# Integer cross attention of a decoder kernel: 128-row scores from queries beside zeros, and the first half of the scores issued twice

## The chip, the cores and the metric

The kernel runs on one core of a Trainium2 chip. The metric is the device time of one execution in microseconds, from the first to the last instruction and the little around them; lower is better. TensorE is written PE, VectorE DVE, ScalarE ACT, GpSimd POOL and SyncE, which issues the DMAs, SP.

## What is computed

The program is a decoder of four layers on `x` of shape (4, 256, 256) in float32, each layer with a self attention, a cross attention on `ctx_2048` (4, 256, 256) and a feed-forward block. The change touches only the cross attention of the second layer (stage "l1x"). Its reference, cut to what matters:

```python
q = (x @ Wq + bq).reshape(1, B * N, 16, 16)          # 1024 queries, 16 heads of 16
kv = (cond @ Wkv + bkv).reshape(1, -1, 2, 16, 16)    # 1024 keys and values
q, k, v = q * 0.25, kv[:, :, 0], kv[:, :, 1]
q = fq_sym(q, axis=-1)     # round to whole numbers -127..127 times a scale
k = fq_sym(k, axis=-1)
v = fq_sym(v, axis=2)
attn = softmax(q @ k.T)
attn = fq_unsigned(attn)   # whole numbers 0..255 times a scale
out = (attn @ v) @ Wp + bp
```

Every query of the four batches attends to all 1024 keys.

## The kernel before, in words

The 1024 queries are 8 tiles of 128 rows, and a tile has 16 heads, so the stage is 128 steps, numbered n = 16·tile + head; a head of its tile is called step h below. At line 1567 `at(n)` gives both. What a step does, engine by engine:

- **PE** (`tensor`, lines 1607 to 1642). Two products (line 1618) write the scores of one head, 128 queries by 1024 keys, into one of three double banks `wide[n % 3]`. The stationary operand is the tile's turned queries, the moving one the turned keys `kt`. A head takes 64 rows of these, four slots of 16: the whole-number query is repeated in each slot, and the slots of the key hold the scaled key cut into three bfloat16 parts and zeros. Two heads share the 128 rows, so the products take rows 0 to 63 for an even head and 64 to 127 for an odd one (`r`, line 1610). A score waits for the exponentials of step n-3 (line 1616), which free its bank. Then PE mixes the values of step n-7 (line 1628): eight products of 128 rows and 16 columns, which wait for POOL's whole probabilities (line 1623). At h = 9 of the next tile it turns a finished tile's output (line 1632), at h = 11 it multiplies it with `Wp` (line 1637, four float32 products of 256 columns) once ACT has copied the turned output (line 1754). PE takes all of this in this one order. The products are issued in the helper at line 101, the transposes in the one at line 107.
- **DVE** (`vector`, lines 1680 to 1707): the maximum over 1024 scores (line 1684) and a small operation on it (line 1686); at h = 7 the reciprocal and scaling of the tile before (lines 1689, 1694); at h = 12 the sum into the residual and its statistics (lines 1699 to 1703).
- **ACT** (`scalar`, line 1748): the exponentials of 1024 scores as bytes, and the copy of line 1754. After every second tile it normalizes a batch for the block that follows (line 385).
- **SP** (`sync`, lines 1813 to 1823): turns the bytes by a DMA transpose (line 1823), once exponentials n and POOL's step n-6 are done. At h = 4 it turns the next tile's queries (line 1797) by another transpose.
- **POOL** (`gpsimd`, lines 1783 to 1793): widens the turned bytes to bfloat16 (line 1787, "whole"), adds a bias at h = 4 (line 1791), and at h = 7 after every second tile it computes the normalization's scale (lines 346 to 358), for which it waits for DVE's statistics of h = 12.

Each engine's program is written in order, with waits on semaphores; there is no planner in this stage. After the loop the items of the following feed-forward block run (PE lines 1640 to 1642: float32 products of 256 columns). Queries lie in `arena_a`, two buffers of 512 words per row; the untransposed keys `kx` lie in `big_b` and are dead once the keys are turned (line 1800).

Of the kernel before, what the change touches and what calls it, by code (L numbers as in the profile page):

```python
# [11 lines left out]
BF16 = mybir.dt.bfloat16  # L12
# [6 lines left out]
P = 128  # L19
NB, S, D = 4, 256, 256  # L20
TB = S // P
NT = NB * TB
CB = TB * D
KH = D // P
H = 16
# [105 lines left out]
def build(nc, d, out):  # L131
# [1388 lines left out]
    def l1_cross():  # L1520
        s = "l1x"
# [4 lines left out]
        mx, ls, rl = wk.take(NT * H), wk.take(NT * H), [wk.take(H) for _ in range(2)]  # L1526
        c = Cut(arena_a)
        kt = [c.take(NT * P, BF16) for _ in range(H // 2)]
        qt_ = [c.take(H // 2 * P, BF16) for _ in range(2)]
        ca = Cut(arena_a, c.at)  # L1530
        nf = l1x_nf
        kr = [ca.take(512) for _ in range(NB)]
# [56 lines left out]
        def tensor():  # L1589
            def queries(b):  # L1590
                t.wait_ge(*(yield xt_a, s, b))
                for i in range(TB):
                    ins = products(t, banks[4 + b].f[:, i * D:(i + 1) * D], with_row(xt, b, i, lambda k: W["wq4"][:, k * D:(k + 1) * D], W["bq4"]))
                ins.then_inc(*ts.up(s, "q", b))

            yield from queries(0)
            yield from norm_tensor(s, nf, last_bank, [3], by_scalar=True)
            yield from queries(1)
            yield from queries(2)
            yield from queries(3)  # L1600
            for k in range(KH):
                t.wait_ge(*(yield vs, s, "values", k))
                for c in range(2):
                    z = 2 * k + c
                    turns(t, id_b, [(banks[z].h[:, i * P:(i + 1) * P], vq[:, value_keys(k * 2048 + c * 512, i)]) for i in range(4)]).then_inc(*ts.up(s, "vi", z))
            yield MEET
            for n in range(N + 14):
                if n < N:
                    i, h = at(n)
                    r = slice(64 * (h % 2), 64 * (h % 2) + 64)  # L1610
                    if h == 0:
                        t.wait_ge(*(yield q_t_d[i % 2], s, i))
                    if i == 0 and h % 2 == 0:
                        t.wait_ge(*(yield k_t_d[h // 2], s))
                    if n >= 3:
                        t.wait_ge(*(yield exped, s, n - 3))
                    for c in range(2):
                        ins = products(t, wide[n % 3][:, c * 512:(c + 1) * 512], [(qt_[i % 2][r, h // 2 * P:(h // 2 + 1) * P], kt[h // 2][r, c * 512:(c + 1) * 512])])
                    ins.then_inc(*scored.up(s, n))
                if 0 <= n - 7 < N:  # L1620
                    u = n - 7
                    i, h = at(u)
                    t.wait_ge(*(yield gs, s, "whole", u))
                    if h == 0 and i >= 2:
                        t.wait_ge(*(yield added, s, i - 2))
                    if h == 0 and i >= 3 and i % 2:
                        t.wait_ge(*(yield xt_a, "l1f", (i - 3) // 2))
                    products(t, out_bank(i)[:, h * HD:(h + 1) * HD],
                             [(pt[u % 6][:, j * P:(j + 1) * P], vi[:, h * HD + j * D:h * HD + j * D + HD]) for j in range(NT)]).then_inc(*mixed.up(s, u))
                if (i := ended_at(n - 10)) is not None:  # L1630
                    t.wait_ge(*(yield normed_o, s, i))
                    turns(t, id_f, [(out_bank(i)[:, D + j * P:D + (j + 1) * P], oc[i % 2][:, j * P:(j + 1) * P]) for j in range(KH)]).then_inc(*o_in_psum.up(s, i))
                if (i := ended_at(n - 12)) is not None:
                    t.wait_ge(*(yield o_t_a, s, i))
                    if i == 0:
                        t.wait_ge(*(yield as_, s, "weights"))
                    products(t, out_bank(i)[:, 0:D], [(ot[i % 2][:, j * P:(j + 1) * P], wp[j]) for j in range(KH)]).then_inc(*out_made.up(s, i))
                if (b := batch_ended_at(n - 19)) is not None:
                    yield from norm_tensor("l1f", big_a, odd_bank, [b], by_scalar=True)
                if n in (128, 132):  # L1640
                    yield from some(items_tensor, 1)
            yield from some(items_tensor, ALL_ITEMS)
# [117 lines left out]
        def gpsimd():  # L1760
# [22 lines left out]
            for n in range(N):  # L1783
                g.wait_ge(*(yield p_t_d[n % 6], s, n))
                if n >= 6:
                    g.wait_ge(*(yield mixed, s, n - 6))
                g.tensor_scalar(pt[n % 6].rearrange("p (j e q) -> p j e q", j=NT // 2, e=2), by_byte(p8[n % 6]), 1.0, 0.0,  # L1787
                                ALU.mult, ALU.add).then_inc(*gs.up(s, "whole", n))
                if n % H == 4:
                    x_i = x[:, n // H * D:(n // H + 1) * D]  # L1790
                    g.tensor_tensor(x_i, x_i, W["bp4"], ALU.add).then_inc(*gs.up(s, "bias", n // H))
# [2 lines left out]
            yield from ffn_gpsimd()  # L1794

        def turn_queries(i):
            sp.dma_start(qt_[i % 2].rearrange("p (r q) -> p r q", r=H // 2), qx[:, i * 1024:(i + 1) * 1024], transpose=True).then_inc(*q_t_d[i % 2].up(s, i))

        def turn_keys(pr):
            sp.dma_start(kt[pr].rearrange("p (i c) -> p i c", i=NT), kx[:, pr * 1024:(pr + 1) * 1024], transpose=True).then_inc(*k_t_d[pr].up(s))  # L1800
# [1 line left out]
        def sync():  # L1802
# [10 lines left out]
            for n in range(N):  # L1813
                i, h = at(n)
                if h == 4 and i + 1 < NT:
                    sp.wait_ge(*(yield gs, s, "spread", (i + 1) // TB))
                    if i:
                        sp.wait_ge(*(yield scored, s, i * H - 1))
                    turn_queries(i + 1)
                sp.wait_ge(*(yield exped, s, n))  # L1820
                if n >= 6:
# [1940 lines left out]
```

## Time and profile before

| | |
|---|---|
| median of 3 runs | 1644.3 us (1640.3 to 1646.01) |
| the profiled execution | 1643.9 us, span 1642.6 us |
| mean granted PE clock over the span | 0.891 of 2.4 GHz |
| busy | PE 1428.1 us (87%), DVE 1096.7 (67%), ACT 796.2 (48%), POOL 752.1 (46%) |
| the 128 steps, first score to last maximum | about 615 to 823 us |
| maximum over the scores, L1684 | x128, 1214 ns each |
| exponentials, L1748 | x128, 1204 ns each |
| bytes to whole numbers, L1787 | x128, 1045 ns each |

Times in the profile count from the first instruction. A PE matmul is pipelined: its duration holds its way through the array, and in a run of matmuls the next one starts before the last has ended, so what a matmul costs is read from the starts. The granted clock is 1.00 for 2.4 GHz and 0.50 for 1.2 GHz. "Idle before" names what released an engine that had stood still.

### The profile page before, as it was taken

The numbers are of one execution on the slowest core, as the hardware profiler recorded it, in microseconds if no ns is written. First come the engines' busy times: TensorE is split into PE (matmuls) and PEld (weight loads), VectorE is DVE, ScalarE is ACT, GpSimd is POOL, SyncE is SP. The second block draws the span as 40 slices with busy tenths as digits, with TensorE's granted clock in tenths as the row PEclk, the third lists the DMA queues.
The fourth block names the chain that finished last, engine by engine and source line by source line (L and its number), as shares of the span: only waits on it lengthen the run. The fifth ranks groups of instructions, "written<-read, shape, count | busy, mean of one in ns | idle before, by whom it ended". The sixth has DMA issues, their size and how long they took to land. (4 is left out here: it accounts for less than half of the span.)

```text
span 1642.6 us, 25782 instructions
## 1 busy us (share of the span) xinstructions
PE 1428.1 (87%) x8360; PEld 1030.2 (63%) x8360; DVE 1096.7 (67%) x2831; ACT 796.2 (48%) x2003; POOL 752.1 (46%) x1214
## 2 busy tenths in 40 slices
PE   6999997889999988999999698556888777789999
PEld 4666764578888852333377587434666555568887
DVE  6877776357677669889845735675866588954222
ACT  3444442143434358788721624456777477741111
POOL 3888882056656646766712122434656423320000
PEclk9999997899999995555599899769999989999999
DMA  7000002100000016555450000020423264310000
GB/s 274 26 8 8 1 1 77 45 15 7 1 8 1 1 27 116 92 98 85 89 197 1 0 1 0 4 109 15 64 53 60 45 154 108 61 14 1 7 7 13
DMA packets 168836, 77.87 MB, mean 47 GB/s; under 512 B 156928, under 2 KB 161408, under 8 KB 167552
## 3 DMA queue, kind: packets, MB, share of 16 engines
q1 hardware_dynamic: 168704, 76.23, 19.9%
q8 instruction: 68, 1.11, 0.3%
q14 instruction: 64, 0.52, 0.1%
HBM read 37.40 MB, written 1.05 MB: 23 GB/s over the span
## 5 line engine op out<-in xcount | busy, mean ns | idle before, releaser
L101 PE MATMUL banks<-normed_t,arena_a 128*128 128x256 f32 x1120 | 257.3, 385 | 2.5 <-PEq L3667 2.5
L464 POOL TENSOR_TENSOR lut_weights<-lut_weights,arena_b 128x536 f32<-128x536 f32 x128 | 181.5, 1418 | 122.3 <-DVE arena_b L454 113.1
L101 PEld LDWEIGHTS banks<-normed_t,arena_a 128*128 128x128 f32 x1120 | 215.3, 193 | 33.0 <-issue 3.1
L596 POOL TENSOR_SCALAR work<-work,small 128x256 f32<-128x256 f32 (+1 forms) x384 | 175.1, 474 | 41.8 <-DVE small L588 41.8
L101 PE MATMUL banks<-arena_a 64*128 64x512 bf16 (+1 forms) x384 | 163.4, 545 | 16.4 <-ACT arena_a L1748 8.4
L1748 ACT ACTIVATE arena_a<-banks,work 128x1024 uint8<-128x1024 f32 x128 | 154.0, 1204 | 42.3 <-DVE work L1686 36.0
L1684 DVE TENSOR_REDUCE work<-banks 128x1 f32<-128x1024 f32 x128 | 155.4, 1214 | 19.5 <-PE banks L101 19.4
L1787 POOL TENSOR_SCALAR arena_a<-arena_a 128x1024 bf16<-128x1024 uint8 x128 | 132.3, 1045 | 55.0 <-DMA arena_a<-arena_a 54.8
L107 PE MATMUL banks<-identity,work 128*128 128x128 f32 x1000 | 139.1, 281 | 19.7 <-ACT work L541 6.2
L576 ACT ACTIVATE work<-banks,small 128x256 f32<-128x256 f32 (+1 forms) x258 | 114.8, 453 | 69.0 <-DVE small L563 55.4
L107 PEld LDWEIGHTS banks<-identity,work 128*128 128x128 f32 x1000 | 115.7, 144 | 41.9 <-issue 15.2
L1900 DVE TENSOR_TENSOR big_b<-big_b,banks 128x512 f32<-128x512 f32 (+2 forms) x48 | 30.8, 642 | 136.1 <-PE banks L101 126.2
L346 POOL TENSOR_SCALAR rstd<-mean_var 128x2 f32<-128x2 f32 x48 | 9.6, 200 | 225.0 <-DVE mean_var L417 156.5
L101 PEld LDWEIGHTS bank<-work,arena_a 128*128 128x128 bf16 x1024 | 37.1, 106 | 109.6 <-POOL arena_a L1787 67.5
L101 PE MATMUL banks<-arena_a,normed_t 128*128 128x192 f32 (+3 forms) x352 | 97.8, 424 | 5.4 <-PEq L3667 5.3
L1914 ACT ACTIVATE big_b<-banks 128x512 f32<-128x512 f32 (+2 forms) x48 | 26.8, 559 | 153.1 <-PE banks L101 153.0
L101 PEld LDWEIGHTS banks<-arena_a,normed_t 128*128 128x128 f32 x352 | 57.3, 198 | 37.3 <-issue 34.6
L541 ACT COPY work<-banks 128x512 f32<-128x512 f32 (+1 forms) x96 | 52.9, 551 | 45.1 <-PE banks L107 44.2
L101 PE MATMUL banks<-arena_a,big_a 128*128 128x256 f32 x320 | 72.8, 380 | 2.0 <-ACT big_a L3100 1.5
L101 PE MATMUL bank<-arena_a,big_b 128*128 128x256 f32 x288 | 70.1, 387 | 4.8 <-DVE big_b L2212 2.8
L576 ACT ACTIVATE work<-bank,small 128x256 f32<-128x256 f32 (+1 forms) x126 | 56.3, 454 | 33.7 <-DVE small L563 27.2
L2848 ACT CAST big_a<-big_b 128x192 bf16<-128x192 f32 (+1 forms) x192 | 54.6, 334 | 30.9 <-POOL big_b L2857 13.9
(467 smaller groups left out, 3187.7 us busy)
## 6 DMA issues: line engine op xcount, KB each, us to landing
arena_a<-in_L3f_wg SPq DMA_DIRECT2D x8, 512.0 KB, 3.9
arena_b<-in_lut_idx SPq DMA_DIRECT2D x8, 268.0 KB, 3.2
arena_b<-in_L_wqn SPq DMA_DIRECT2D x4, 512.0 KB, 10.2
arena_b<-in_L_wo SPq DMA_DIRECT2D x4, 512.0 KB, 13.0
arena_a<-in_L_wq SPq DMA_DIRECT2D x1, 2048.0 KB, 7.5
arena_a<-in_L_wo SPq DMA_DIRECT2D x1, 2048.0 KB, 12.5
arena_a<-arena_a SPq DMA_TRANSPOSE x128, 2.5
arena_b<-in_L2f_gv SPq DMA_DIRECT2D x1, 2048.0 KB, 7.9
```

The lines of the kernel that those rows point to most:

```text
L101: ins = t.matmul(out, lhs_t, rhs, start=start and i == 0, stop=stop and i == n - 1)
L107: ins = t.transpose(out, src, ident[0:src.shape[0], 0:src.shape[0]])
L464: g.tensor_tensor(o, o, lut_t[j % 2], ALU.add).then_inc(*summed.up(c * LUT + j))
L541: a.copy(A.pt[(2 * n + 1) % 4][:, 0:c], banks[5].f[:, 0:c]).then_inc(*p_t_a.up(A.s, n))
L576: ins = a.activation(e[:, c], src[:, c], ACT.Exp, bias=A.mx[k][:, 2 * hh + i:2 * hh + i + 1], scale=A.scale, accum_out=A.ls[k][:, 2 * hh + ...
L596: ins = g.tensor_scalar(e[:, c], e[:, c], A.rl[n % 2][:, 2 * hh + i:2 * hh + i + 1], 0.0, ALU.mult, ALU.add)
L1684: v.tensor_reduce(mx[:, z:z + 1], wide[n % 3], AX.X, ALU.max).then_inc(*vs.up())
L1748: a.activation(eb[n % 6].bitcast(U8), wide[n % 3], ACT.Exp, bias=mx[:, n:n + 1], scale=sq[:, n:n + 1], accum_out=ls[:, n:n + 1]).then_inc( ...
L1787: g.tensor_scalar(pt[n % 6].rearrange("p (j e q) -> p j e q", j=NT // 2, e=2), by_byte(p8[n % 6]), 1.0, 0.0, ALU.mult, ALU.add).then_inc(* ...
L1900: ins = v.tensor_tensor(o[r, cols], o[r, cols], (banks[pair].f if r.start else up)[r, cols], ALU.mult)
L1914: ins = a.activation(F.hidden(q)[dst, cols], banks[F.pair(q)[0]].f[src, cols], ACT.Silu)
L2848: ins = a.copy(q5[:, i, :, lo:hi, :], src.broadcast_to([P, HG, hi - lo, HD]))
```

## The change

From the second tile on, a tile's queries are turned twice, into two buffers in the dead key region `big_b`. In buffer e POOL then writes zeros over the 64 rows that belong to the heads of the other parity. A score product now takes all 128 rows of query buffer and keys, where the zeros cancel the other head's keys. Before the two score products PE issues the first of them once more, with the same operands and the same destination, so the result is the same. The first tile stays as it was.

```diff
-        qt_ = [c.take(H // 2 * P, BF16) for _ in range(2)]
+        qt_ = c.take(H // 2 * P, BF16)
+        cz = Cut(big_b)
+        beside_zeros = [[cz.take(H // 2 * P, BF16) for _ in range(2)] for _ in range(2)]
...
                     if h == 0:
-                        t.wait_ge(*(yield q_t_d[i % 2], s, i))
+                        t.wait_ge(*(yield (gs, s, "zeros", i) if i else (q_t_d[0], s, 0)))
...
+                    if i == 0:
+                        q_, k_ = qt_[r, h // 2 * P:(h // 2 + 1) * P], kt[h // 2][r, :]
+                    else:
+                        q_, k_ = beside_zeros[i % 2][h % 2][:, h // 2 * P:(h // 2 + 1) * P], kt[h // 2]
+                        products(t, wide[n % 3][:, 0:512], [(q_, k_[:, 0:512])])
                     for c in range(2):
-                        ins = products(t, wide[n % 3][:, c * 512:(c + 1) * 512], [(qt_[i % 2][r, h // 2 * P:(h // 2 + 1) * P], kt[h // 2][r, c * 512:(c + 1) * 512])])
+                        ins = products(t, wide[n % 3][:, c * 512:(c + 1) * 512], [(q_, k_[:, c * 512:(c + 1) * 512])])
...
+                if n % H == 8 and n // H + 1 < NT:
+                    i = n // H + 1
+                    g.wait_ge(*(yield q_t_d[i % 2], s, i))
+                    for e in range(2):
+                        g.wait_ge(*gs.now())
+                        g.memset(beside_zeros[i % 2][e][64 * (1 - e):64 * (2 - e), :], 0.0).then_inc(*gs.up())
+                    gs.all(s, "zeros", i)
+                    g.wait_ge(*gs.now())
...
         def turn_queries(i):
-            sp.dma_start(qt_[i % 2].rearrange("p (r q) -> p r q", r=H // 2), qx[:, i * 1024:(i + 1) * 1024], transpose=True).then_inc(*q_t_d[i % 2].up(s, i))
+            for to in beside_zeros[i % 2] if i else [qt_]:
+                sp.dma_start(to.rearrange("p (r q) -> p r q", r=H // 2), qx[:, i * 1024:(i + 1) * 1024], transpose=True).then_inc(*q_t_d[i % 2].up(s, i))
...
                     if i:
                         sp.wait_ge(*(yield scored, s, i * H - 1))
+                    else:
+                        for pr in range(4):
+                            sp.wait_ge(*(yield k_t_d[pr], s))
                     turn_queries(i + 1)
```

So per tile from the second: 16 more score products, 32 score products of 128 rows in place of 64, one more DMA transpose on SP at h = 4, two memsets on POOL at h = 8 (after its whole numbers of that step), and PE's wait at h = 0 of the tile is for the memsets.

## Rows read from the trace of the kernel before

**Rows 1.** The page's 40 slices of the span: the granted clock in tenths.
```profile
PEclk9999997899999995555599899769999989999999
```

**Rows 2.** A stretch of the stage: us, then PE, PEld, DVE, ACT, POOL busy; clock; DMA share.
```profile
668.00:694.00 26.00, 23.99 (x168) 8.12 (x168) 23.37 (x38) 21.13 (x34) 17.01 (x21) 0.50 0.52 92
```

**Rows 3.** Order of time in an even step of the third tile: start, duration, engine, line, operation.
```profile
668.51 1.22 DVE L1684 TENSOR_REDUCE work<-banks 128x1 f32<-128x1024 f32 x1
...
668.60 1.03 PE L101 MATMUL banks<-arena_a 64*128 64x512 bf16 x2
668.63 1.20 ACT L1748 ACTIVATE arena_a<-banks,work 128x1024 uint8<-128x1024 f32 x1
...
669.89 1.21 DVE L1684 TENSOR_REDUCE work<-banks 128x1 f32<-128x1024 f32 x1
```

**Rows 4.** Waits between the engines, 616 to 826 us: total, times, longest.
```profile
DVE work L1684 <- PE banks L101: 19.4, 14, 2.0
```

**Rows 5.** Order of time around h = 11 of the third tile.
```profile
682.86 0.36 ACT L1754 COPY arena_b<-bank 128x256 f32<-128x256 f32 x1
...
683.27 2.08 PE L101 MATMUL bank<-arena_b 128*128 128x256 f32 x4 [0.29 <-ACT arena_b L1754]
...
685.28 1.03 PE L101 MATMUL banks<-arena_a 64*128 64x512 bf16 x2
...
686.35 1.23 DVE L1684 TENSOR_REDUCE work<-banks 128x1 f32<-128x1024 f32 x1 [1.96 <-PE banks L101]
...
686.56 1.03 PE L101 MATMUL banks<-arena_a 64*128 64x512 bf16 x2
```

**Rows 6.** The last steps and the items after them, in order of time.
```profile
822.27 6.74 PE L101 MATMUL banks<-normed_t,lut_weights 128*128 128x256 f32 x16 [0.90 <-ACT arena_a L1748]
...
828.64 1.07 PEld L101 LDWEIGHTS bank<-work,arena_a 128*128 128x128 bf16 x32
```

**Rows 7.** The same products at the full clock: a stretch of the last block, three bf16 products.
```profile
1540.00:1550.00 10.00, 10.00 (x48) 8.80 (x47) 2.95 (x6) 1.19 (x2) 0.00 (x0) 1.00 0.00 0
...
1101.49 0.59 PE L101 MATMUL banks<-arena_a,big_b 128*128 128x512 bf16 x2
1101.92 0.38 PE L101 MATMUL banks<-arena_b 128*128 128x512 bf16 x1
1102.14 0.59 PE L101 MATMUL banks<-arena_a,big_b 128*128 128x512 bf16 x2
```

**Rows 8.** A stretch in which the clock came back (columns as in rows 2), and its products.
```profile
289.10:292.50 3.40, 2.73 (x13) 2.32 (x12) 0.17 (x1) 0.59 (x1) 0.00 (x0) 0.50 0.77 328
292.50:296.00 3.50, 3.50 (x18) 2.58 (x18) 1.76 (x14) 0.26 (x1) 0.00 (x0) 0.99 0.00 0
...
L101 PE MATMUL banks<-arena_b,normed_t 128*128 128x136 f32 x23 | 6.3, 446 | 2.1 <-ACT normed_t L370 1.4 <-DVE normed_t L366 0.8
```

**Rows 9.** POOL, PE and DVE around the start of the fourth tile, in order of time.
```profile
690.32 8.11 POOL L1787 TENSOR_SCALAR arena_a<-arena_a 128x1024 bf16<-128x1024 uint8 x8
...
691.74 1.03 PE L101 MATMUL banks<-arena_a 64*128 64x512 bf16 x2
...
697.63 1.23 DVE L1684 TENSOR_REDUCE work<-banks 128x1 f32<-128x1024 f32 x1 [0.53 <-PE banks L101]
```

**Rows 10.** The nearest memset on POOL, in a later stage: duration, start, form.
```profile
L2515 POOL MEMSET arena_b<- x1: 944/944/944, 1070.9 to 1070.9; 128x1024 bf16 x1
```

**Rows 11.** POOL's whole numbers of step 8, and the score of step 16.
```profile
637.70 1.04 POOL L1787 TENSOR_SCALAR arena_a<-arena_a 128x1024 bf16<-128x1024 uint8 x1 [0.28 <-DMA arena_a<-arena_a]
...
639.12 1.03 PE L101 MATMUL banks<-arena_a 64*128 64x512 bf16 x2
```

**Rows 12.** SP's transposes in order of time, and a wait that its lateness causes.
```profile
629.41 22.24 SPq L1823 DMA_TRANSPOSE arena_a<-arena_a  x16
651.74 1.26 SPq L1797 DMA_TRANSPOSE arena_a<-big_a  x1
...
646.90 1.23 DVE L1684 TENSOR_REDUCE work<-banks 128x1 f32<-128x1024 f32 x1 [1.02 <-PE banks L101]
```

## The prediction

> **What bounds the kernel now.** I read the granted clock by slices first. It is at 9 tenths or more almost everywhere, and at 5 in the four slices that hold this stage [rows 1]: TensorE runs at 1.2 GHz there and at 2.4 GHz around it. A stretch of it shows that this is no matter of an idle engine: PE is busy 24.0 of 26 us, 92%, and the clock stays at 0.50 [rows 2].
>
> The order of time in one step [rows 3] gives the bound. From one maximum to the next it is 669.89 - 668.51 = 1.38 us, the 1.22 us operation and the small one behind it, without a gap: DVE sets the step. Where PE runs without waiting, its next scores start 686.56 - 685.28 = 1.28 us after the last [rows 5]; so it follows DVE with 0.10 us to spare. Over a tile DVE needs 16 x 1.38 = 22.1 us, and 0.62 at h = 7 and 1.02 at h = 12 for its other work: 23.7 us.
>
> A tile takes more, because DVE waits for PE: 19.4 us in 14 waits, the longest 2.0 us [rows 4]. The long one stands at h = 11 to 12 of a tile [rows 5]: ACT's copy ends at 683.22, PE starts the four products with `Wp` at 683.27, the scores of h = 12 can start only at 685.28, and DVE starts 1.96 us late at 686.35. At 1.2 GHz the chain from product to maximum is 3.08 us. So the stage is bound by DVE with a PE stall of 2.0 us in each of tiles 1 to 7.
>
> **The change, part by part.** The sum is made against the profiled execution, 1643.9 us (span 1642.6), 0.4 below the median of the three runs, 1644.3.
>
> *Does the clock rise?* The only thing in this stage that differs in kind from stretches at 2.4 GHz is the shape: scores of 64 rows, mixing of 16 columns. In the stretch in which the clock came back, PE was busy only 2.73 of 3.40 us, less than here, but its products were 128 rows high [rows 8]; the 23 products of 136 columns are the bulk of it. The change makes all score products 128 rows high and issues three for two. I take it that the clock rises, some microseconds after the second tile begins, and mostly holds. The Trainium skill (TensorE: Matmul & The Clock Gate, § What's actually happening) says that the gate's ratio is set by how busy the PE has been recently. By busy share alone this stage should have been at 2.4 GHz all along; [rows 2] speaks against that reading, and if busy share were all, padding rows would change nothing and the third product would be pure cost (second rival below).
>
> *Price of a step at 2.4 GHz.* Three bf16 products of 512 columns start within 1102.14 - 1101.49 = 0.65 us, and the last takes 0.38 us to its end; 48 float32 products of 256 columns fill 10 us, 0.208 each [rows 7]. So a triple is ready 2 x 0.22 + 0.38 = 0.82, say 0.86 us after its start, where two at half clock took 685.28 to 686.35 = 1.07 [rows 5]. The step stays at DVE's 1.38.
>
> *The stall at h = 11.* Four products 0.85 instead of 2.01, scores 0.86 instead of 1.07: 1.7 for 3.08 us, 1.34 less. Seven tiles: **-9.4**. A stall of 0.6 to 0.7 stays, since ACT's copy isn't earlier.
>
> *The tail.* The 16 products after the last score take 822.27 to 828.64 = 6.4 us at half clock [rows 6]; at 0.208 each they take 3.3. Some of this is given back because the mixing behind them then waits for POOL's last whole numbers: **-2.5**.
>
> *Two smaller waits.* Soon after their start tiles 3, 5 and 7 have a DVE wait of 0.53 us [rows 9] and about 0.1 around it, behind ACT's normalization, which the next item swallows: **-1.9**. The 1.02 us wait in tile 1 [rows 12], PE behind a late transpose, falls into slack that the next items make: **-1.1**.
>
> *The memsets, and what PE waits for now.* Each is 64 rows of 1024 bf16; the nearest row is 944 ns for 128 rows of 1024 [rows 10], so two cost 1.9, with their waits 2.05 us. Bounds: half of it, were height to count, and 2.05. I take 2.05. In most tiles POOL is at h = 8 long before PE needs the queries, 8 steps later, and it costs nothing. But after every second tile POOL has waited at h = 7 for DVE's statistics of h = 12: whole numbers of h = 8 start at 690.32 and end at 691.36, the scores of h = 0 of the next tile start at 691.74 [rows 9]. With the memsets the zeros are there at 693.4; scores 1.7 us late, of which 0.2 is regained by the quicker product: 1.5 us in tiles 3, 5 and 7: **+4.4**. The same at tile 1: whole numbers of step 8 end at 638.74, step 16's scores started at 639.12 [rows 11]. **+1.6**.
>
> *The second query transpose.* SP in backlog issues 16 transposes in 22.24 + 0.09 us, 1.40 each, and one query transpose takes 1.35 [rows 12]. A tile costs SP 16 x 1.40 + 2 x 1.35 = 25.1 us, 1.35 more than now, where the new tile is about 24.4 (23.7 + 0.65) plus the waits above. So SP, idle now for part of each tile, comes to its limit. In the first tile it already is late (x16 without a gap [rows 12]), and the extra transpose there lands on the path: **+1.35**. In tiles 2 to 7 the queue stands about 3 us late after h = 4; PE mixes only seven steps later, which hides about that much. Bounds: nothing, and per tile the 1.02 us that such lateness costs in [rows 12]. I take 0.3 in six tiles: **+2**.
>
> *The clock again.* Tile 1 begins at 1.2 GHz, where a step with three products costs 1.28 + 0.43 = 1.71 instead of 1.38; three steps: **+1**. The new 1.5 us waits in tiles 3, 5 and 7 can let the clock fall for a stretch, two or three steps of +0.33 each; bounds 0 and 1 in each of the seven tiles: **+1.2**.
>
> Sum: -9.4 - 2.5 - 1.9 - 1.1 = -14.9; +4.4 + 1.6 + 1.35 + 2 + 1 + 1.2 = +11.5; together **-3.4**, 1643.9 to 1640.5.
>
> **Rivals.**
> First, *the added waits are hidden*: POOL's memsets of 64 rows are cheap, SP's lateness stays inside the seven steps and the clock never falls. Then +4.4 becomes 1.5, +1.6 becomes 0.6, +2 and +1.2 vanish: about -11, 1633. For it: POOL is busy 17.0 of 26 us [rows 2], so it catches up. Against it: a step of DVE leaves it 0.33 us.
>
> Second, on the other side, *the clock stays at 1.2 GHz*: the zeros or the repeated product don't count for the gate. Then PE is the bound: 16 x 1.71 + 2.01 = 29.4 us a tile against 23.7 + 2.0 = 25.7, +3.7 in seven tiles and +1.35 in the first, 1671. It decides from the point where PE's step passes 1.38. For it: PE is busy 92% and the clock stays down [rows 2]. Against: [rows 8].
>
> Third, *the clock comes and goes*: each wait of over a microsecond (h = 0 of tiles 3, 5, 7; late transposes) drops it, and it is back only after several steps at 1.71, with the products of h = 11 caught at half clock in some tiles. Half of the steps at +0.33 is +18 where PE is the bound, less the slack: 6 to 14 us on top of my sum, around 1652.
>
> That the change doesn't do what it says is no case here: the operands and counts are fixed by the code.
>
> **How the numbers follow.** About 0.3%, 4.9 us, is what a measurement can tell from no change. My forecast, the clock rises and the waits cost about what they sum to, has a chance of 0.60, and with its bounds it spans 1634 to 1647: about a third of it is faster than 1639.4, nearly all else within. Hidden waits 0.17 (faster). Clock at 1.2 GHz 0.10 (slower). Coming and going 0.13, mostly slower. Faster: 0.20 + 0.17 = 0.37; same 0.39 + 0.03 = 0.42; slower 0.21. The likeliest time is 1640.5. The range 1632 to 1655 leaves out the second rival and the edges of the first and third.
>
> **What the profile would show.** Right: the granted clock 1.00 from about 648 us to the end of the stage; triples of 128-row products; the four products of h = 11 in 0.9 us and DVE's idle before h = 12 at 0.6 to 0.7; tiles of about 24.4 to 26.2 us; PE idle before h = 0 of tiles 1, 3, 5 and 7, released by a POOL memset of about 0.94 us; SP almost without a gap. Wrong: memsets near 0.5 us, or PE waits at h = 0 absent; a clock of 0.50 in most stretches and 1.71 us between scores; PE waiting for POOL's whole numbers by more than a microsecond in every tile.

## The result and the profile after

The changed kernel took 1649.3 us (median of 20 runs, 1644.5 to 1663.9) against 1644.4 us before (20 runs, 1638.8 to 1653.6): ratio 1.0033, interval 1.0018 to 1.0048. That is slower by just over 0.3%, about 4.8 us, where 3.4 us faster was forecast. The profiled execution took 1650.5 us, its span 1649.2. A run more than 1.5% above the fastest of its kernel is a slow one, and two such runs, one of e2 and one of x5 below, are left out wherever a mean is given.

The clock did rise. The page's row of the granted clock in 40 slices, against [rows 1]:

```profile
PEclk9999997899999996999999899769999889999999
```

The stage in stretches (columns as in [rows 2]):

```profile
642.00:668.00 26.00, 19.63 (x169) 9.82 (x172) 21.74 (x33) 20.43 (x33) 19.20 (x20) 0.76 0.69 106
668.00:694.00 26.00, 18.13 (x199) 10.30 (x201) 24.53 (x43) 21.85 (x34) 19.40 (x20) 1.00 0.62 105
694.00:720.00 26.00, 18.12 (x182) 10.13 (x186) 22.73 (x37) 21.52 (x37) 20.13 (x23) 0.93 0.57 99
720.00:746.00 26.00, 18.84 (x179) 9.84 (x182) 23.75 (x38) 21.24 (x34) 18.90 (x19) 0.87 0.61 104
```

PE does half as much again in score products and is busy 18 us of 26 where it was busy 24; from the second tile to the eighth it runs 31 us at 1.2 GHz in place of 182. Yet DVE waits for PE no less than in [rows 4]. The waits from 616 to 830 us (total, times, longest):

```profile
DVE work L1691 <- PE banks L101: 22.1, 16, 3.0
PEld banks L101 <- POOL big_b L1801: 10.5, 6, 1.8
PE banks L101 <- POOL big_b L1801: 8.9, 5, 2.1
```

The end of the third tile and the start of the fourth in order of time, against [rows 5, 9]:

```profile
689.30 0.36 ACT L1761 COPY arena_b<-bank 128x256 f32<-128x256 f32 x1
...
689.71 1.13 PE L101 MATMUL bank<-arena_b 128*128 128x256 f32 x4
...
691.53 1.22 DVE L1691 TENSOR_REDUCE work<-banks 128x1 f32<-128x1024 f32 x1 [0.70 <-PE banks L101]
...
695.49 1.04 POOL L1794 TENSOR_SCALAR arena_a<-arena_a 128x1024 bf16<-128x1024 uint8 x1
...
696.66 1.95 POOL L1801 MEMSET big_b<- 64x1024 bf16 x2
...
698.66 1.34 PE L101 MATMUL banks<-arena_a,big_b 128*128 128x512 bf16 x3 [1.71 <-POOL big_b L1801]
...
700.04 1.23 DVE L1691 TENSOR_REDUCE work<-banks 128x1 f32<-128x1024 f32 x1 [1.92 <-PE banks L101]
```

At h = 11 the wait of 1.96 is 0.70. At the next tile's start the zeros come late, and the triple behind them takes 1.34 us where one at 2.4 GHz takes 0.82 (684.69 in the same trace): the clock stood at 1.2 GHz from 698.8 to 702.2 us, right behind PE's pause of 1.71 us. In all three profiles of the changed kernel it falls within 3 us of the first maximum of tiles 3, 5 and 7, each of which has such a pause ahead of it. What one place gives, the other takes.

The memsets in the view of their line (duration min/median/max, first and last start, form):

```profile
L1801 POOL MEMSET big_b<- x14: 944/946/946, 644.3 to 804.2; 64x1024 bf16 x14
```

A second look at the whole: I call **the stage** the time from the first maximum (L1684) to the last addition of the residual. It takes 220.7 us before and 221.5 after (both ends are the starts of the instructions). In this one profile 4.0 us more had gone before its start, which two further profiles of the changed kernel do not show (below), and behind it there are 807.5 us against 805.6. So the stage alone doesn't explain the loss.

### The profile page after: what moved, and what is told of

Same layout as the page of the kernel before. It is cut to its first block and busy times, and to the rows that moved or that the text cites. A ratio compares the mean times of both kernels' runs of the same rounds, so it can differ in the third digit from the quotient of the medians.

```text
span 1649.2 us, 26007 instructions
## 1 busy us (share of the span) xinstructions
PE 1392.4 (84%) x8443; PEld 1045.8 (63%) x8472; DVE 1094.8 (66%) x2831; ACT 796.7 (48%) x2003; POOL 765.0 (46%) x1228
## 5 line engine op out<-in xcount | busy, mean ns | idle before, releaser
L464 POOL TENSOR_TENSOR lut_weights<-lut_weights,arena_b 128x536 f32<-128x536 f32 x128 | 181.3, 1417 | 123.6 <-DVE arena_b L454 114.4
L101 PE MATMUL banks<-arena_a,big_b 128*128 128x512 bf16 x371 | 115.4, 415 | 47.8 <-ACT arena_a L1755 35.7
L101 PEld LDWEIGHTS banks<-arena_a,big_b 128*128 128x128 bf16 x400 | 32.4, 102 | 76.6 <-ACT arena_a L1755 38.0
L101 PEld LDWEIGHTS bank<-work,arena_a 128*128 128x128 bf16 x1024 | 43.8, 99 | 53.6 <-POOL arena_a L1794 29.1
```

Of the source, the lines that this page charges most:

```text
L101: ins = t.matmul(out, lhs_t, rhs, start=start and i == 0, stop=stop and i == n - 1)
L464: g.tensor_tensor(o, o, lut_t[j % 2], ALU.add).then_inc(*summed.up(c * LUT + j))
```

## The experiments

Each edited kernel gave one profile and 4 to 12 runs in all. **Stage** is read from the profile. **Outside** is the mean of its runs, less 1.3 us around the span, less the stage; its error is that of the mean and doesn't hold the spread of the stage. The runs of the kernel before were timed beside the others, in five groups. **Half clock outside** comes from the granted clock of each run: 2 x (1 - clock) x span, less what the profile has in the stage. The last column is from the profile: where the granted clock first falls between 310 and 450 us behind the last addition. Kernels e2, x3 and x4 leave out part of the computation; their times serve to separate causes. Kernels e1 to e7, x4 and b1 to b3 are edits of the changed kernel or of its parts, x1 to x3 and x5 edits of the one before; "products" is how many more PE has than before.

| kernel | products | runs | median | ratio, interval | stage | outside | half clock outside | fall |
|---|---|---|---|---|---|---|---|---|
| before | 0 | 132 | 1644 to 1647 | 1 | 220.7 | 1423.5 +-0.5 | 148 | none |
| after | +112 | 22 | 1649.3 | 1.0033 (1.0018, 1.0048) | 221.5 | 1427.7 +-1.0 | 161 | 379 |
| e1 | +112 | 12 | 1645.0 | 1.0004 (0.9977, 1.0031) | 219.0 | 1425.3 +-1.5 | 164 | 382 |
| e2 | +112 | 12 | 1644.2 | 0.9982 (0.9950, 1.0014) | 212.1 | 1429.7 +-2.0 | 160 | 382 |
| e3 | 0 | 10 | 1649.9 | 1.0033 (1.0000, 1.0065) | 224.9 | 1424.1 +-2.0 | 130 | none |
| e4 | +112 | 4 | 1674.7 | 1.0159 (1.0119, 1.0198) | 248.5 | 1424.1 +-1.8 | 156 | 380 |
| e5 | 0 | 10 | 1649.1 | 1.0007 (0.9980, 1.0034) | 224.2 | 1423.0 +-1.2 | 146 | none |
| e6 | 0 | 10 | 1652.1 | 1.0046 (1.0018, 1.0073) | 227.1 | 1425.3 +-1.6 | 154 | none |
| e7 | +224 | 6 | 1688.9 | 1.0276 (1.0238, 1.0314) | 254.2 | 1435.0 +-2.6 | 188 | 381 |
| x1 | +112 | 12 | 1649.5 | 1.0018 (0.9988, 1.0049) | 220.9 | 1427.1 +-1.5 | 162 | 380 |
| x2 | +224 | 12 | 1648.6 | 1.0011 (0.9991, 1.0030) | 221.1 | 1427.5 +-0.9 | 162 | 380 |
| x3 | -112 | 12 | 1653.0 | 1.0023 (0.9995, 1.0051) | 220.6 | 1429.7 +-1.9 | 160 | 343 |
| x4 | 0 | 12 | 1641.4 | 0.9977 (0.9950, 1.0004) | 217.2 | 1424.0 +-1.8 | 142 | none |
| x5 | +128 | 12 | 1644.9 | 0.9989 (0.9961, 1.0018) | 220.9 | 1420.8 +-1.6 | 141 | none |
| b1 | +96 | 12 | 1644.2 | 0.9986 (0.9963, 1.0009) | 216.4 | 1426.4 +-1.2 | 165 | 378 |
| b2 | +96 | 12 | 1648.9 | 1.0016 (0.9988, 1.0044) | 221.5 | 1426.9 +-1.4 | 161 | 380 |
| b3 | +128 | 12 | 1641.0 | 0.9980 (0.9950, 1.0010) | 214.6 | 1425.5 +-1.1 | 150 | none |

### The stage: the clock and what raises it

**r1, r2, r3** are repeats, of the kernel before (r1) and of the changed one.

> The kernel before once more, for a second profile: how much the parts of the span that the change doesn't touch vary by themselves. The stage, first maximum to last sum into the residual, should again take 220 to 222 us, as its clock is 0.50 throughout; the 616 us before it and the 806 us behind it may move by some microseconds, by the clock in the stretches where it comes and goes.

> The changed kernel once more. Theory D (the whole kernel's +5 us is the stage: its waits fall differently into the clock from run to run, and the first profile, +0.8 us, was a lucky one): stage 222 to 228 us. Theory E (it lies outside the stage, in chance or in what the stage leaves behind): stage within 1 us of 221.5 again, with the +5 in the 806 us behind it.

> As the run before it: a third profile of the changed kernel, so that the spread of its stage time is seen. D: 222 to 228 us and differing by over 1 us between profiles. E: 221 to 222.

Measured: 1641.4, 1644.1 and 1650.5 us; the stage 220.5, 220.9 and 221.0; its start at 614.5, 614.2 and 614.0. So the stage repeats within 0.6 us, the 4 us ahead of it in the first profile were chance, and behind it stand 805.1, 807.7 and 814.3.

**e1**: the memsets at h = 6, not 8.

```diff
-                if n % H == 8 and n // H + 1 < NT:
+                if n % H == 6 and n // H + 1 < NT:
```

> The changed kernel with POOL's two memsets at h = 6 instead of h = 8, so ahead of the wait for DVE's statistics at h = 7. Theory A (the loss is the zeros coming late behind that wait: DVE idle 1.9 to 2.0 us at the start of tiles 3, 5 and 7, and the clock falls in them): these three waits vanish and most falls with them, and tiles 3, 5 and 7 begin without a gap; 6 to 8 us below the changed kernel, so about 1641 to 1643, 1 to 4 below the kernel before. Theory B (the loss is SP's second query transpose): little moves, 0 to 2 us below the changed kernel, waits of over 1.5 us for late bytes stay in every tile. In tile 1 the zeros come late all the same (POOL is there late because SP is).

Measured: stage 219.0. The stalls at the starts of tiles 1 and 3 are gone, those of tiles 5 and 7 are 1.53 in place of 2.12. But the first tile stays at 27.6: it now has a stall of 1.81 at its last step, where PE waits for the whole numbers that POOL makes behind the two memsets. Tile 1 has one of 3.1 at h = 11, tile 2 one of 1.77 and tile 6 one of 1.64. Some 2 of the 6 us that late zeros cost come back, not the 6 to 8 of theory A.

**e2**: no zeros and one query transpose a tile; the other head's rows hold queries, so the scores are the sums of two heads.

```diff
+                    q_, k_ = (qt_[i % 2][:, ...], kt[h // 2]) if i else (qt_[0][r, ...], kt[h // 2][r, :])
...
-                    g.memset(beside_zeros[...]..., 0.0)
```

> The kernel before, but from the second tile on the score products take all 128 rows of the one query buffer and of the keys, and the first is issued twice: no second transpose, no memsets. Left out: the zeros, so each score also holds the other head's products (the time of the exponentials and maxima doesn't depend on the values). It is what the change would bring if its zeros cost nothing. Theory A and B alike (the clock works as forecast, the zeros' making is the loss): clock 1.00 from about 650 us on with few falls, the stall at h = 11 at 0.7 instead of 2.0 us in tiles 1 to 7, tail 3 us shorter: 10 to 13 us below the kernel before, 1631 to 1635. Theory C (the clock itself brings less than forecast): less than 6 us below. If real values in the rows, rather than zeros, mattered to the clock, its granted clock would differ from the changed kernel's beyond the stalls.

Measured: stage 212.1, 8.6 us below before, between theories A and C: all that the clock gives. In the whole time it doesn't show (ratio 0.9982, interval 0.9950 to 1.0014), because outside the stage e2 has 6 us more than before. A stretch of it (columns as in [rows 2]):

```profile
668.00:694.00 26.00, 16.62 (x185) 9.58 (x185) 24.60 (x41) 22.18 (x35) 17.57 (x21) 1.00 0.61 102
```

and in its order of time h = 12 of the third tile:

```profile
688.79 1.22 DVE L1687 TENSOR_REDUCE work<-banks 128x1 f32<-128x1024 f32 x1 [0.70 <-PE banks L101]
```

In five of the seven tiles this step comes 0.78 late by the distance of the maxima (2.04 before); in tiles 1 and 3, where the clock fell at 661.5 and 712.7 us, on the steps around h = 11, it is 2.10 and 1.71. The chain of h = 11 is where a fall hurts.

**e3**: the change without the repeated product.

```diff
-                        products(t, wide[n % 3][:, 0:512], [(q_, k_[:, 0:512])])
```

> The changed kernel without the repeated product: two score products of 128 rows. If 128 rows are enough for the clock, it is granted 2.4 GHz as in the changed kernel and the time is the same or 1 to 2 us less. If the repeat is needed, the clock stays at 0.50 in nearly all of the stage, PE's step stays at 1.28 us, and the time is that of the kernel before plus the zeros' costs: +6 to +12 us, 1650 to 1656.

Measured: stage 224.9, nine falls of the clock and 144 us at 1.2 GHz in the tiles 1 to 7. The padded rows alone are not enough; the repeat is needed.

**e4**: 64-row products, issued three times as in the change, without zeros.

```diff
-                        q_, k_ = beside_zeros[i % 2][h % 2][:, ...], kt[h // 2]
+                    q_, k_ = qt_[i % 2][r, ...], kt[h // 2][r, :]
```

> The kernel before with its first 64-row score product issued twice from the second tile on, nothing else. If the height of the products matters to the clock, it stays at 0.50 through the stage, PE becomes the bound at 1.71 us a step and the time is 24 to 30 us above the kernel before, 1668 to 1674. If a busy PE is enough, the clock rises within a few microseconds of the second tile and the time is 8 to 13 us below the kernel before.

Measured: stage 248.5, 29.8 to 30.7 us a tile, close to the 29.4 of the second rival. A stretch of it:

```profile
694.00:720.00 26.00, 26.00 (x163) 8.93 (x162) 20.66 (x32) 18.80 (x30) 16.59 (x20) 0.50 0.41 79
```

PE without a gap, at 1.2 GHz; e2, whose product counts are the same and whose rows alone differ, has it busy 16.62 of 26 us at 2.4 GHz.

**e7**: before, with two extra 128-row products of mixed heads ahead of the two real 64-row ones (the result is the reference's).

```diff
+                    if i:
+                        for c in range(2):
+                            products(t, wide[n % 3][:, ...], [(qt_[i % 2][:, ...], kt[h // 2][:, ...])])
```

> The kernel before, but from the second tile on PE first issues both products of a score with all 128 rows of the query buffer and keys, into the same bank, and then the two true products of 64 rows, which overwrite them. No zeros, no second transpose, no memsets; the result is the reference's. If the cause of the changed kernel's loss is the making of the zeros (A), this keeps the clock without it: PE's step at 2.4 GHz is some 1.2 us, under DVE's 1.38; stage 212 to 215 us against 220.7, the whole 5 to 9 us below the kernel before. Its risk: at 1.2 GHz a step is 1.28 + 0.85 = 2.13 us and half the products are low, so the clock may rise only at the float32 products of h = 11, and until then each step costs 0.75 us more; if it doesn't hold, the stage is 230 to 250 us.

Measured: stage 254.2, above the 230 to 250 of its risk. Two tiles of 34.4 us went by, all but some 7 us of each at 1.2 GHz, PE being the bound at 2.15 us a step; later the clock came and went. Padding beside the real work costs more than it returns.

**e5** prices the second transpose, **e6** the memsets, both at 1.2 GHz on the kernel before.

```diff
+            for to in [spare[i % 2], qt_[i % 2]] if i else [qt_[0]]:
```

> The kernel before with every query transpose from the second tile's on issued twice (the first into a place that nobody reads), and with the wait for the key transposes in the first tile; no zeros, no wider or repeated scores, so PE's program is as long as before. My sum gave the second transposes 1.35 us in the first tile and 0.35 a tile in six others: stage 220.5 + 1.35 + 2 = 224, first tile 25.4. If the 3.5 us that the change added in the first tile are all its transposes: first tile 27.5. By theory F the rest behind the stage stays at 805 us; by theory G as well.

```diff
+                if n % H == 8 and n // H + 1 < NT:
...
+                        g.memset(spare[e][64 * (1 - e):64 * (2 - e), :], 0.0).then_inc(*gs.up())
```

> The kernel before with the two memsets of a tile in POOL's order at h = 8 (into a place that nobody reads) and PE's wait for them before the next tile's first score; one transpose a tile, scores as before, the clock stays at 1.2 GHz. My sum priced the late memsets at 1.5 us in the tiles 3, 5 and 7 and 1.6 in tile 1: stage 220.5 + 6 = 226.5. If the stalls of 2.0 us that the change shows there come from the clock falling in PE's pause, the same memsets here, where there is no higher clock to lose, give 1.5 or less; if they come from POOL alone, 2.0 again (stage 228.5). Behind the stage 805 us by theory F.

Measured: e5's stage is 224.2, +3.5: 1.46 in the first tile, 1.04 in the second, 0.33 in the third and 0.67 in the sixth. e6's is 227.1, +6.4. Its start of the fourth tile:

```profile
698.01 1.95 POOL L1799 MEMSET big_b<- 64x1024 bf16 x2
700.06 1.01 PE L101 MATMUL banks<-arena_a 64*128 64x512 bf16 x2 [1.75 <-issue]
701.11 1.22 DVE L1688 TENSOR_REDUCE work<-banks 128x1 f32<-128x1024 f32 x1 [1.65 <-PE banks L101]
```

The step is 1.7 us late at the tiles 1, 3, 5 and 7, and 1.96 to 2.12 in the changed kernel. Both kernels issue these scores at 1.2 GHz, two products in 1.01 us here and three in 1.34 there, and that is the difference; at 2.4 GHz the three would have taken 0.82.

### Outside the stage: the length of PE's program

After e7 the two kinds stood apart: kernels with 112 more products seemed to lose some microseconds in stretches whose instructions are the same. Theory F put that to the number of instructions, theory G to the warm clock of the stage, rival H to chance. **x1** adds the products and nothing else.

```diff
+                    if i:
+                        products(t, wide[n % 3][:, 0:8], [(qt_[i % 2][r, ...], kt[h // 2][r, 0:8])])
```

> The kernel before with one more instruction for each score from the second tile: a product of 64 rows by 8 columns into the place that the real score then overwrites; 112 more instructions of PE, as in the change, and nothing else of it. The result is unchanged. In the stage it should cost nothing (220.5 us from the first maximum to the last residual addition, as before). Theory F, that the longer program of PE moves something behind the stage: 809 to 811 us from the last residual addition to the end (before: 805), a fall of the granted clock some 75 us after the one at 1140 us, a median 4 to 5 us above before. Theory G, that what happened in the stage (its clock, its heat) sets what comes behind: 805 us behind it and a median equal to before within 1.5 us.

Measured: stage 220.9, outside 1427.1 against 1423.5, and a fall 380 us behind the last addition. The same 3.4 us at that place (columns as in [rows 2]), before:

```profile
1216.20:1219.60 3.40, 1.52 (x16) 1.27 (x16) 0.96 (x3) 2.73 (x9) 2.38 (x7) 1.00 0.15 28
```

in x1:

```profile
1215.40:1218.80 3.40, 3.40 (x23) 2.04 (x21) 1.71 (x5) 3.23 (x14) 1.13 (x3) 0.50 0.01 2
```

and in the changed kernel:

```profile
1221.00:1224.40 3.40, 3.40 (x22) 2.19 (x21) 1.44 (x4) 3.23 (x14) 0.81 (x2) 0.51 0.01 2
```

**x2** has 224 tiny products; **x3** is before without the last 128 keys in the heads' outputs from the second tile; **x4** is the changed kernel with the same left out.

```diff
-                             ... for j in range(NT)]).then_inc(*mixed.up(s, u))
+                             ... for j in range(NT - (i > 0))]).then_inc(*mixed.up(s, u))
```

> The kernel before with two more tiny products (64 rows by 8 columns) for each score from the second tile: 224 more instructions of PE. Theory F (the number of PE's instructions ahead of the rest of the program shifts what comes behind): the time outside the stage rises again, 1423 for before, 1427 with 112 more, so 1430 to 1435 here (e7, with 224 more, had 1435); the median 8 to 12 us above before, of which at most 2 inside the stage. Rival H (the 112 more instructions did nothing and the kernels differ outside the stage by chance alone): outside 1423 to 1427.

> The kernel before without the last of the eight products of each head's output from the second tile (so the last 128 keys are left out of these outputs): 112 fewer instructions of PE, scores and transposes as before. The stage is set by VectorE's steps, so it should stay at 220 to 221 us. Theory F: outside the stage 1419 to 1421 us on the mean, or 1423 if fewer instructions don't undo anything. Rival H: 1423.

> The changed kernel without the last of the eight products of each head's output from the second tile (the last 128 keys are left out of these outputs), so that PE has as many instructions as in the kernel before. Theory F: outside the stage 1423 us on the mean in place of the 1428 of the change, and a mean of 1645 to 1646. Theory G (the warm clock or the shifted stage sets what comes behind) and rival H put it at the 1427 to 1428 of the change, a mean of 1649 to 1650. The stage itself 219 to 221.5 (PE a little less busy, perhaps another fall of the clock).

Measured: x2 1427.5 and x3 1429.7 outside, x4 1424.0. The theory that more instructions cost more fell: fewer cost as well, and 224 no more than 112 in x2 (e7, with 224 as well, has 1435.0, which stays unexplained). x4 speaks against the warm clock as the cause: its stage is as warm as the changed kernel's (27 us at 1.2 GHz in tiles 1 to 7), its program as long as before's, and it has neither the fall nor the longer time. What was left: any length other than before's, or the place of the instructions in their transfers. The pages' instruction queue (packets, MB, share), before:

```profile
q8 instruction: 68, 1.11, 0.3%
```

in x3, and in x2:

```profile
q8 instruction: 67, 1.10, 0.3%
```

```profile
q8 instruction: 70, 1.15, 0.3%
```

The trace of before has 17563 records of PE, so 258 a packet; 128 products, two records each, are one packet. **x5** has 128 tiny products.

```diff
+                        for _ in range(2 if i == 1 else 1):
+                            products(t, wide[n % 3][:, 0:8], ...)
```

> The kernel before with 128 tiny products (64 rows by 8 columns) in the stage, one for each score from the second tile and a second one in the second tile. A product is two instructions in the trace (a weight load and a matmul), and PE's 17563 records fill 68 transfers of the instruction queue, 258 a transfer, so 128 products are very nearly one whole transfer more. Theory K (what matters is where PE's instructions lie in these transfers, not how many there are): no fall of the granted clock 380 us behind the last addition, 1423 to 1424.5 us outside the stage on the mean, a mean of 1646. Theory L (any length but that of before costs, or chance): the fall is there and 1426 to 1428 outside, a mean of 1649 to 1650, as with x1, x2 and x3.

Measured: 1420.8 outside, and at the place of the fall

```profile
1217.60:1221.00 3.40, 1.73 (x18) 1.42 (x18) 1.33 (x3) 3.40 (x14) 1.23 (x4) 1.00 0.01 2
```

Theory K had forecast the missing fall, and 1423 to 1424.5. So it is the place that matters and not the length, as far as one whole transfer can tell; 256 or 258 records aren't told apart, and no other whole number of transfers was tried. Together: the eight profiles of seven kernels with 0 or 128 more products have no fall there, the eleven with 96, 112 or 224 have one at 378 to 382 us. Each kernel of the first kind has 130 to 154 us at half clock outside the stage, each of the second, x3 with them, 156 to 188. Weighted by their errors, the six edited kernels with 0 or 128 products have 1423.9 +-0.6 outside, the ten others, the changed one with them, 1427.4 +-0.4: 3.5 us. Taken against the runs of the kernel before that were timed beside them, the six have 0.5 +-0.7 more and the others, without the changed one, 3.4 +-0.6.

The profiles show where it is lost. I take the time between the same two instructions of DVE, the 435th and the 850th from the last addition on, some 335 and 515 us behind it. It is 177.8 to 181.3 us in the eight profiles, 182.0 to 186.5 in the eleven and 188.9 in x3; the means of the first two kinds differ by 4.1 +-0.7. At 355 us the two kinds are level (0.4 +-0.5), at 362 the eleven are 1.9 us ahead, and at 515 they are 3.8 +-0.7 behind. From 362 to 515 us the eight have 7 to 17 us at half clock and the eleven 24 to 31.

One link of the way there can be seen. In a stretch of 20 us, 12 to 32 us ahead of the place of the fall, the transposes behind L2866 (as it is numbered before) in x5:

```profile
L2869 SPq DMA_TRANSPOSE lut_weights<-big_a x4: 1232/1290/1349, 1192.1 to 1201.9; - x4
...
  PE banks L2884: 2.6, 1
...
DMA to landing us min/median/max: 3.2/3.4/4.8
```

and in x1:

```profile
L2868 SPq DMA_TRANSPOSE lut_weights<-big_a x4: 1232/1333/1683, 1189.9 to 1198.6; - x4
...
  PE banks L2883: 0.9, 1
DMA to landing us min/median/max: 3.2/3.4/3.6
```

They are issued in pairs, 1.3 us apart, and mostly land 3.1 to 3.6 us after their issue. One of the first pair lands after 4.8 to 5.1 and PE waits 2.3 to 2.7 us for it in all eight profiles without the fall; in all eleven with it the wait is 0.9 to 1.1, which is why they are ahead at 362. The packets of PE's instruction queue (q8) in the traces say why it is late. In the eight such a transfer starts 2.7 to 3.0 us after that transpose was issued, while it is on its way. In the eleven the next transfer starts 4.0 to 6.7 us after the issue of that pair's second transpose, when both have landed. This holds for the program as a whole: of its 64 transposes lut_weights<-big_a in each of 20 profiles, 145 had a transfer of PE's instructions start 1.2 to 3.2 us after their issue, and 103 of these took 4.4 us or more to land, 4.65 at the median; of the 1135 others 9 did, and the median is 3.22. (I chose the bounds 1.2, 3.2 and 4.4 on seeing the times.) So the place of PE's instructions decides which transpose is late. How that leads to the fall behind it isn't shown: x3 has the late transpose and the 2.8 us wait, and loses time all the same, with its fall at 343.

### Versions meant to be faster

**b1**: the change from the third tile; transposes at h = 2, one memset at h = 4 and one at h = 6.

```diff
-                if n % H == 8 and n // H + 1 < NT:
+                if n % H in (4, 6) and 2 <= n // H + 1 < NT:
...
-                if h == 4 and i + 1 < NT:
+                if h == (2 if i else 4) and i + 1 < NT:
```

> A version meant to be faster, with the reference's result: the change begins at the third tile (the second keeps 64-row scores and one transpose, so the first tile loses nothing), the two transposes go out at h = 2 and the memsets stand at h = 4 and h = 6, so no score waits for them. From e2's stage of 212.1 us, in which there are no zeros and the second tile is repeated too: stage 212 to 215, tiles 2 to 7 of 24.5 to 26, first tile 24.0, no stall at h = 15 over 0.5. Behind the stage by theory F about 809 to 810 us (96 more instructions of PE), so a median of 1644 - 7 + 5 = 1642; by theory G, if the warm stage is what costs behind it, the same; if neither holds, 1637.

**b2**: its two transposes at h = 1 and 3.

```diff
-                if h == (2 if i else 4) and i + 1 < NT:
+                if i + 1 < NT and h in ((4,), (5, 7), (1, 3))[min(i, 2)]:
```

> As b1 (the change from the third tile, zeros ahead of the need), with the two query transposes of a tile put one at h = 1 and one at h = 3 (h = 5 and 7 for the third tile's), so that the transposes of the exponentials wait for 1.3 us twice rather than 2.6 at once. In b1 the stage took 216.4 us, with stalls of 1.1 to 1.3 at h = 15 and 1.5 at n = 25. If those come from the transposes standing one behind the other: stage 212 to 214.5, mean 1640 to 1642. If they come from the memsets or the clock: 216 again, mean 1644.

**b3**: b1 with 32 tiny products in the second tile, for a whole packet.

```diff
+                        for _ in range(2 * i):
+                            products(t, wide[n % 3][:, 0:8], [(qt_[1][r, ...], kt[h // 2][r, 0:8])])
```

> b1 (the change from the third tile, the zeros ahead of the need) with 32 tiny products in the second tile, so that PE has 128 products more than before, one whole transfer of instructions. The stage as in b1, 216.4 us, and up to 0.5 more. Theory K: outside the stage 1423.5 in place of b1's 1426.4, no fall at 380 us behind the last addition, a mean of 1641. Theory L: b1's 1426 to 1427, a mean of 1644 to 1645.

Measured: b1's stage is 216.4, its first tile 24.1, and the longest wait for zeros 0.8 us; its second tile is 28.8, 1.9 more than before. Outside it has the 1426 of its kind. The 212 to 215 expected for its stage was missed. b2 is a miss too: 221.5, with stalls of 3.9 at the end of tile 1 and 3.7 in tile 4. Its stage is from one profile, so the split can't be told from chance, but the pair of transposes gets no support as the cause. b3: stage 214.6, no fall behind it, as theory K had it, and a median of 1641.0 us against 1644.7 for the kernel before, timed beside it. Its time outside the stage, 1425.5 +-1.1, doesn't decide between the theories: K expected 1423.5, L 1426 to 1427, and b1 has 1426.4. Its mean is 1641.4 +-1.1, 2.9 +-1.7 us below the 23 runs of before beside it and 4.1 below all 132; the interval of the ratio, 0.9950 to 1.0010, includes no change, so that b3 is faster isn't shown.

## Why the prediction was wrong

The direction was wrong: -3.4 us forecast, +4.8 measured. That the time lies inside the range is owed to the range's width and not to the sum, half of whose error stands outside everything that the prediction weighed. The sum failed in two places of about the same size.

**A term was missing: outside the stage, +4.** The sum took the rest of the program as unchanged because its instructions are. It is 1427.7 us against 1423.5. The same comes with x1, which adds 112 tiny products and nothing else, and goes away in x4 and x5, by the place of PE's instructions in their transfers; between the same two instructions, 335 and 515 us behind the last addition, it is 4.1 +-0.7 us. Nothing in the rows read pointed to it.

**In the stage: -3.4 forecast, +0.5 measured** (221.1 on the mean of three profiles, 220.6 before on two).
- *Does the clock rise?* Right, and for the reason given: e4 and e2 separate height from busy share. The Trainium skill (TensorE: Matmul & The Clock Gate, § What's actually happening) ties the gate to how busy the PE was; e4, with PE busy 26.00 of 26 us and a clock of 0.50, doesn't bear that out as a rule on the busy share alone.
- *Costs.* Right. Memsets +4.4 and +1.6, measured 6.4 at 1.2 GHz (e6); second transpose +1.35 and +2, measured 1.46 in the first tile and 3.5 in all (e5): together 9.9 us against 9.35. The first tile's 3.5 us in the changed kernel (27.5 for 24.0) are nearly those of e5 and e6, 1.46 and 1.81. The value taken for a memset, 944 ns as for 128 rows [rows 10], was right. Between e2 and the changed kernel, at 2.4 GHz, both together are 9.0.
- *Gains, less the clock's own terms.* This step failed: -9.4 - 2.5 - 1.9 - 1.1 + 1 + 1.2 = -12.7, and e2, which has these (but not the late zeros, on which part of the +1.2 was put), gives -8.6. The term of h = 11, -9.4, came to -6.6. Where the clock held, its size was nearly right: 1.26 a tile for 1.34, or for 1.37, as the prediction's own 3.08 less 0.85 and 0.86 has it. But two tiles of e2 had fallen clocks there and gained 0.3 and nothing. The tail gave 1.6 in e2 for 2.5 (1.4 to 3.1 in the changed kernel's profiles), the first tile took 0.3 more, and the four small terms came to -0.7 for -0.8. "The clock again" priced a fall at two or three steps of 0.33; it should have been priced where PE is the bound: at h = 11, where it takes back the whole 1.3, and behind late zeros, where PE's pause brings it about.
- *The rival "comes and goes"* had the mechanism: 4 to 6 falls, some caught at h = 11. It priced them at 6 to 14 us on top of the sum. What the runs lay to them is 2.3 us at h = 11 in e2 and 0.3 at each of four starts of a tile in the changed kernel (1.96 to 2.12 against e6's 1.7).

What the profile should show came out: triples, 0.70 at h = 12, PE's waits for POOL at the start of tiles 1, 3, 5 and 7. SP's lateness was there, though tile by tile it fell unevenly.

## What to carry to other kernels

Price a gain that hangs on a state (here the clock) at the places where the engine is the bound, and ask there what happens when the state drops out for one step; slack hides the drop everywhere else. When a change alters how many instructions an engine has, time a kernel with only that number changed, and look in the trace where the transfers of its instructions fall: here it was worth 3 to 4 us of 1645 in stretches that nobody touched, and in b1 it hid most of an improvement of 4.3 us in the stage. Where a rewrite needs cleared or doubled inputs, put them a good way ahead of their use and start it one tile later than the first tile in which the queue is late already.

## What the runs showed of the hardware

- 64-row bf16 products left TensorE at 1.2 GHz even when it was busy 26.00 of 26 us (e4); 128-row products held 2.4 GHz at 16.62 of 26 (e2), but not when each half of the scores was issued once (e3, 0.57 in a stretch with PE busy 20.01 of 26).
- The time of a run goes with its mean granted clock: over the 132 runs of the kernel before, 0.35 us more for each us more at half clock outside the stage. The spread of single runs, 5.2 us, is 1.8 when that is taken out.
- PE's instructions come by DMA, a transfer for some 258 of its records, and such a transfer delays a DMA transpose on its way: the transposes lut_weights<-big_a landed after 4.65 us at the median where one started 1.2 to 3.2 us behind their issue (145 of them in 20 profiles), after 3.22 otherwise (1135). The transposes arena_a<-arena_a of the stage show nothing of it, 2.49 against 2.46.
- Adding 96, 112 or 224 products to PE's program moved the late transpose, and a fall of the clock came 378 to 382 us behind the stage; with 0 or 128 more (256 records, about a whole transfer) neither happened. With 112 fewer (x3) the transpose was late as before and the fall came at 343.
